# A hand-ordered two-layer attention kernel: a new first image, and small moves in each later turn

## The reference, cut to what matters

```
layer 0, per image x [256, 1024]
  q = Wq x + bq, k = Wk x + bk        (32 rows each)
  v = Wv x + bv                       (256 rows)
  attn = softmax over j of q_i . k_j
  x1 = gamma * (v attn^T) + x
layer 1, per image x1 [256, 1024]
  h = group_norm(x1) (32 groups of 8 channels)
  q, k, v = projections of h (256 rows each)
  attn = softmax(q . k / 16)
  y = x1 + Wproj (v attn^T) + bproj
```

## Time and profile before

| | us |
|---|---|
| median of 3 runs | 840.06 (836.66 to 841.46) |
| the profiled execution, its own time | 842.42 |
| its span in the profile | 840.6 |
| PE busy | 789.0 (94%), 3756 matmuls |
| DVE busy | 556.8 (66%) |
| ACT busy | 471.2 (56%) |
| POOL busy | 166.7 (20%) |

### The profile page before, as it was taken

One profiled execution on the slowest core, in us unless ns is written; L12 is line 12 of the kernel. 1 busy time (PEld: TensorE's weight loads), 2 busy tenths in 40 slices (PEclk: granted clock), 3 DMA queues, 4 the chain that ended last, 5 costly groups with the idle time before them and its releaser, 6 DMA issues.

```text
span 840.6 us, 9682 instructions
## 1 busy us (share of the span) xinstructions
PE 789.0 (94%) x3756; PEld 645.5 (77%) x3756; DVE 556.8 (66%) x787; ACT 471.2 (56%) x609; POOL 166.7 (20%) x141
## 2 busy tenths in 40 slices
PE   5788887999999989999999999999999999999998
PEld 4567666888788777877778877888778788888786
DVE  5554675677758686676956777586865857385665
ACT  4755663557654576445854657545765457444343
POOL 3600233201310041103310034100421024102300
PEclk9879999899999999999999999999999999999999
DMA  7000001001100011000200002000100001000101
GB/s 225 0 1 2 1 0 51 1 1 40 62 1 1 1 51 51 1 1 1 83 19 1 1 0 101 1 1 1 50 1 1 2 1 50 1 1 1 50 1 51
DMA packets 10365, 18.98 MB, mean 23 GB/s; under 512 B 2128, under 2 KB 3920, under 8 KB 10320
## 3 DMA queue, kind: packets, MB, share of 16 engines
q1 hardware_dynamic: 10320, 18.36, 6.3%
HBM read 9.97 MB, written 8.39 MB: 22 GB/s over the span
## 4 chain that ended last, share of the span: by engine, by line
PE 70%; DVE 20%; ACT 7%; issue 2%; DMA 1%; SPq 0%; ACTq 0%; DVEq 0%
PE ring L524 22%; PE ring L526 21%; PE ring L525 21%; PE ring L534 3%; DVE pt_lo L946 3%; PE ring L544 2%; ACT prob L743 2%; DVE neg_raw L931 2%; DVE bn L989 2%; DVE x_lo L861 2%; DVE neg_max L929 2%; DVE pt_lo L949 1%; DVE h_lo L869 1%; ACT ring L764 1%; DVE res L982 1%
## 5 line engine op out<-in xcount | busy, mean ns | idle before, releaser
L524 PE MATMUL ring<-pt_hi,v_hi 128*128 128x512 f32 x512 | 204.1, 399 | 4.2 <-issue 2.0
L525 PE MATMUL ring<-pt_lo,v_hi 128*128 128x512 f32 x512 | 202.6, 396 | 0.0
L526 PE MATMUL ring<-pt_hi,v_lo 128*128 128x512 f32 x512 | 202.5, 395 | 0.0
L743 ACT ACTIVATE prob<-ring,neg_max 128x1024 f32<-128x1024 f32 x64 | 71.6, 1118 | 179.1 <-DVE neg_max L932 179.1
L931 DVE TENSOR_REDUCE neg_raw<-ring 128x1 f32<-128x1024 f32 x64 | 77.9, 1217 | 86.9 <-PE ring L526 86.9
L465 POOL TENSOR_TENSOR v_lo<-v_f,v_hi 128x512 fp32r<-128x512 f32 x32 | 42.9, 1341 | 440.8 <-ACT v_hi L781 440.8
L524 PEld LDWEIGHTS ring<-pt_hi,v_hi 128*128 128x128 f32 x512 | 97.5, 190 | 26.7 <-issue 3.8
L526 PEld LDWEIGHTS ring<-pt_hi,v_lo 128*128 128x128 f32 x512 | 97.6, 191 | 21.8
L525 PEld LDWEIGHTS ring<-pt_lo,v_hi 128*128 128x128 f32 x512 | 97.8, 191 | 19.3
L524 PE MATMUL ring<-h_hi,query_hi 128*128 128x512 f32 x256 | 101.2, 395 | 5.2 <-DVE spread L967 4.9
L929 DVE TENSOR_REDUCE neg_max<-ring 128x1 f32<-128x1024 f32 x64 | 77.7, 1221 | 42.0 <-PE ring L534 42.0
(11 more groups left out here) (118 smaller groups left out, 1234.5 us busy)
## 6 DMA issues: line engine op xcount, KB each, us to landing
out_y<-res SPq DMA_DIRECT2D x32, 256.0 KB, 2.1
x_in<-in_x SPq DMA_DIRECT2D x7, 1024.0 KB, 4.9
x_in<-in_x SPq DMA_DIRECT2D x2, 512.0 KB, 4.7
h_f<-in_wv_t SPq DMA_DIRECT2D x1, 256.0 KB, 5.2
res<-in_wq SPq DMA_DIRECT2D x1, 256.0 KB, 7.3
res<-in_wk SPq DMA_DIRECT2D x1, 256.0 KB, 7.5
res<-in_wv SPq DMA_DIRECT2D x1, 256.0 KB, 7.9
res<-in_wp_t SPq DMA_DIRECT2D x1, 256.0 KB, 7.8
```

The source lines that it names most:

```text
L524: mm(out, w_hi, m_hi, start=first, stop=False)
L525: mm(out, w_hi, m_lo, start=False, stop=False)
L526: return mm(out, w_lo, m_hi, start=False, stop=last)
L743: activation(prob[:, p % PROBS], ring[:, slot], ACT.Exp, bias=neg_max[:, k % 2:k % 2 + 1], accum_out=row_sum[:, k % 2:k % 2 + 1]).then_inc ...
```

## The change

**The first image.** Row tiles of scores are filled without the value quarters 2 and 3 among them; only the four `weights` products stand between them. The value quarters 0 and 1 of image 0 are copied whole by ACT into `v1_f` (a buffer of layer 1 that is free then), and POOL splits them (`first_values0`). POOL writes image 1's split x into `h_hi`, `h_lo`, the place of the normalised input, so it need not wait until image 0's `x_hi` has been read. `split_weights` and `residual0(0)` stand later in POOL's queue. DVE instead of ACT takes the weight products out of PSUM. A step `opening` has an order of its own on ACT and DVE: both halves of `qk` of image 1 share one slot, with shift and keys parts between. In the eight steps of `keys` tiles of image 0 the scores of image 1 stand in `late` instead of `early`, two banks of the value product come before `sides`, and three value quarters (0.3, 1.0, 1.1, written image.quarter) stand in `sides` in the `keys` tile's slot. The `bias` products stand behind the first `keys` tile. The split of image 2's x is put earlier, and its low part on DVE.

**The second image.** The value products of images 0 and 1 are evacuated in the step that finishes them. Statistics and the normalised input of image 0 come one step later; its two group sums share slots with `qk 2.1` and `value0 2.0`.

**In a turn.** `qk(i+1, 0)` goes from `sides` to `late` of step 0; the first bank of the value product of step 3 comes behind `qk(i+1, 1)` instead of ahead of it; `norm` goes from `late` to the end of `sides`.

```diff
-PLACE = {("qk", 1, 0): 0, ("qk", 1, 1): 3}
+PLACE = {("qk", 1, 0): 2, ("value0", 0, 2): 3, ("value0", 0, 3): 0, ("value0", 1, 0): 0, ("value0", 1, 1): 0}
...
-HOST = {("norm", 0, m): ("qk", 2, m) for m in range(2)}
+HOST = {("qk", 1, 1): ("qk", 1, 0), ("bias", 0, 0): ("value0", 0, 2),
+        ("norm", 0, 0): ("qk", 2, 1), ("norm", 0, 1): ("value0", 2, 0)}
...
+    start, scores, opening = Step(slots=(0, 1, 2, 3)), Step(slots=(0, 1, 2)), Step()
+    start.sides = tiles("qk", 0, (0, 1)) + tiles("value0", 0, (0, 1))
+    scores.late = tiles("scores", 0, (0, 1, 2))
+    for m in range(4):
+        scores.late += tiles("weights", 0, (m,)) + tiles("scores", 0, (3 + m,))
+    scores.late += tiles("scores", 0, (7,))
+    scores.take_weights = True
+    opening.opening = True
+    opening.sides = tiles("qk", 1, (0, 1)) + tiles("value0", 0, (2,))
+    opening.late = tiles("shift", 0, (0,))
+    steps = [Step(("keys", 0, k), (0, 0, k - 2) if k >= 2 else None) for k in range(TILES)]
+    steps[0].sides = tiles("bias", 0, (0,))
+    steps[0].rest = True
+    for k in range(7):
+        steps[k + 1].late = tiles("scores", 1, (k,))
+    steps[3].sides = tiles("value0", 0, (3,))
+    steps[4].sides = tiles("value0", 1, (0,))
+    steps[6].sides = tiles("value0", 1, (1,))
+    steps[6].split_x = steps[7].split_x_lo = 2
+    s8, s9, s10 = Step(None, (0, 0, 6)), Step(None, (0, 0, 7)), Step(("keys", 1, 1))
+    s8.early = tiles("scores", 1, (7,))
+    s8.early_log = 1
+    s8.late = tiles("value0", 1, (2,))
+    s9.sides = tiles("shift", 1, (0,))
+    s9.late = tiles("keys", 1, (0,)) + tiles("value0", 1, (3,))
...
-    s3.statistics = 0
+    s4.statistics = 0
     s4.sides = tiles("qk", 2, (0,))
-    s4.late = tiles("norm", 0, (0,))
-    s5.sides = tiles("qk", 2, (1,))
-    s5.late = tiles("norm", 0, (1,))
+    s5.sides = tiles("qk", 2, (1,)) + tiles("norm", 0, (0,))
     s6.early = tiles("scores", 2, (0,))
-    s6.sides = tiles("value0", 2, (0,))
-    s6.hidden = s6.hidden_lo = 0
+    s6.sides = tiles("value0", 2, (0,)) + tiles("norm", 0, (1,))
+    s7.hidden = s7.hidden_lo = 0
...
-        steps[0].sides = tiles("qk", i + 1, (0,))
+        steps[0].late = tiles("qk", i + 1, (0,))
+        steps[3].banks_first = 0
         steps[3].sides = tiles("qk", i + 1, (1,))
...
-            steps[s].late = tiles("norm", i, (m,)) + steps[s].late
+            steps[s].sides += tiles("norm", i, (m,))
...
-            if _layer == 0:
+            if _layer == 0 and _image >= 2:
                 STEPS[_n + 1].evacuate = (_layer, _image)
...
+        def x_split(i):
+
+            return (h_hi, h_lo) if i == 1 else (x_hi, x_lo)
...
+            def first_values0():
+
+                for m in range(2):
+                    two = slice(2 * m, 2 * m + 2)
+                    pool.wait_ge(S["value0_taken"], m + 1)
+                    link(G.tensor_copy(v0_hi[:, two], v1_f[:, m]))
+                    G.tensor_tensor(v0_lo[:, two], v1_f[:, m], v0_hi[:, two].bitcast(F32),
+                                    ALU.subtract).then_inc(S["value0_first"], 1)
...
             small_things()
+            first_values0()
+            first_split_x()
+            bias_rows()
             pool.wait_ge(S["x0_loaded"], 16)
             pool.wait_ge(x_loaded[0], x_loads(0))
             residual0(0)
-            first_split_x()
-            bias_rows()
             split_weights()
-            split_x(2)
...
+            def opening():
+                log_sums(0)
+                for m in range(2):
+                    query_part(("qk", 1, m))
+                shift_rows(("shift", 0, 0))
+                key_part(("qk", 1, 0))
...
+            def opening():
+                key_part(("qk", 1, 0))
+                shifts(0)
+                key_part(("qk", 1, 1))
+                for m in range(2):
+                    query_part(("qk", 1, m))
```

More of the change, by code:

```diff
@@ L111, in second_image @@
+    s9.sides = tiles("shift", 1, (0,))
+    s9.late = tiles("keys", 1, (0,)) + tiles("value0", 1, (3,))
+    return [start, scores, opening] + steps + [s8, s9, s10]
 def second_image():
@@ L137, in second_image @@
     ones[3].late = tiles("scores", 2, (6,))
-    ones[4].sides = tiles("value0", 2, (2,))
-    ones[4].late = tiles("norm", 1, (0,)) + tiles("scores", 2, (7,))
+    ones[4].sides = tiles("value0", 2, (2,)) + tiles("norm", 1, (0,))
+    ones[4].late = tiles("scores", 2, (7,))
     ones[4].log = ones[5].shifts = 2
-    ones[5].sides = tiles("value0", 2, (3,))
-    ones[5].late = tiles("norm", 1, (1,))
+    ones[5].sides = tiles("value0", 2, (3,)) + tiles("norm", 1, (1,))
     ones[6].sides = tiles("shift", 2, (0,))
@@ L521, in wait, with wait_read @@
                 pe.wait_ge(S[name], n)
+            def wait_read(entry):
+                for got in (entry, GUEST[entry]) if entry in GUEST else (entry,):
+                    wait(*reader(got))
+                    if got[0] == "qk":
+                        wait("key_hi", 2 * got[1] + got[2] + 1)
             def three(out, w_hi, w_lo, m_hi, m_lo, first, last):
@@ L658, in fill @@
                 elif kind == "qk":
-                    last = project_qk(i, m, out)
+                    last = project_qk(i, m, half_place(entry))
                 elif kind == "value0":
@@ L687, in values @@
                     elif before and b % 2 == 0:
[L688 to L690 removed]
+                        wait_read(before)
                     w, cols = slice(ct * P, (ct + 1) * P), half_cols[half]
@@ L816, in _ @@
             for now in STEPS:
+                if now.opening:
+                    opening()
+                    continue
                 logits = now.tile and now.tile[0] == "logits"
@@ L1033, in _ @@
                 for entry in now.sides + now.late:
-                    if entry not in first:
+                    if entry not in first and not now.rest:
                         follow(entry)
@@ L1037, in _ @@
                     split_hidden(now.hidden_lo)
+                if now.take_weights:
+                    take_weights()
+                if now.rest:
+                    project_lo(("value0", 0, 2))
+                    project_lo(("bias", 0, 0))
                 if now.shifts is not None:
```

122 lines of the change are left out of this document (67 added, 55 removed).

## The result

The changed kernel takes **847.15 us** (median of 8 runs, 845.10 to 849.36), the kernel before 841.63 us (median of 8 in the same session, 836.66 to 843.48). The ratio is 1.0071 (95%: 1.0047 to 1.0095): slower by 0.7%, or 5.5 us, where 0.2% faster was forecast. The profiled execution took 845.68 us (span 843.9), 3.3 us more than that of before.

A forecast was written before the change was run, and what follows sets the result against it. Bounds: DVE's queue in a turn; in image 0 an ACT-DVE ring around two PSUM slots, and PE's clock. 3.8 + 1.8 - 0.8 - 6.2 - 0.2 = -1.6 us on 842.4 gives 840.8, as median 838.5; range 831 to 846.

The forecast's parts named there:

- The turn: Turns 2 to 6: DVE idles before the first keys tile's low part, 0.76 us a turn, +3.8 us together.
- The second image and the evacuation: Second image -0.8 us, waits going and new ones coming; image 1's evacuation wait gone, -6.2; its first group sum, -0.2.
- the forecast wait of 1.4 us at `scores(2, 0)`: Second image: PE's scores wait for the reader of the first group sum, 1.4 us.
- Opening and keys steps together: Image 0 up to image 1's first value product, 98.05 us in place of 96.24: +1.8 us, bounds -3.1 to +8.5.
- First exponential at 32.65: Opening: eight row maxima in succession end at 26.6, the path behind stays 6.1 us; 32.65 in place of 37.76, -5.1 us.
- The bound of -1 us: Opening's far bound: GpSimd's two subtractions hold DVE up by 2.1 us each, leaving a gain of 1 us.
- GpSimd's chain: Opening: two value quarters, then image 1's x, from 15.4 to 26.2 us, so that `qk(1, 1)` just finds it.
- 4.85 us to the second exponential: Image 0, first to second keys exponential: 4.05 us, 3.57 of them bias products, plus 0.8 for an even chance of half clock.
- Rounds: 43.1 forecast: Image 0's keys steps: three plain 17.1 us, three with a value quarter 20.8, half clock 3.2, image 2's split 2.0.
- Image 0 falls to 1.2 GHz: Slower rival, chance 0.18: PE bounds image 0's plain steps at 7.4 us against 5.7; +6.7 us, 845.2 us.
- The turn is what it looks like: Faster rival, chance 0.12: PE's waits of 1.65 and 0.49 us count fully, five turns win about 8.8 us; 825.9 us.
- The clock holds: Faster rival, chance 0.19: PE stays at 2.4 GHz in image 0 and the second image, 4.9 us off; 833.6 us.

The follow-up runs named there:

- e1: The kernel before with the turn's three moves alone (`qk(i+1, 0)`, the bank, `norm`); 845.95 us, ratio 1.0048.
- e3: The changed kernel with DVE taking a `qk` entry in `late` ahead of the step's tile again, PE's and ACT's orders kept; 844.52 us, ratio 1.0041.
- e12: The kernel before with two moves of the turn alone (`norm`, the bank behind `qk`), the first half of `qk` left in place; 840.19 us, ratio 0.9989.
- e4: The changed kernel with GpSimd's first residual (image 0) waiting until the shift of image 0 is made; 841.66 us, ratio 1.0001.
- e7: The changed kernel with e4's GpSimd wait, scores 1 to 6 of image 1 in `early`, and the turn of before; 825.49 us, ratio 0.9806.
- e9: e7 with the low part of a later image's x on DVE one step earlier in each turn; 818.37 us, ratio 0.9721.
- e10: e9 with the first scores tile of image 1 early too and image 0's statistics back in their old step; 815.15 us, ratio 0.9689.
- e6: The changed kernel with 13 useless matmuls in PE's two opening waits, 8 before the shift, 5 before the first keys tile; 843.92 us, ratio 1.0024.
- e2: The changed kernel with the turn of before, so the new first and second image alone; 844.12 us, ratio 1.0026.
- e11: The changed kernel with the low part of image i+2's x on DVE one step earlier in each turn; 839.31 us, ratio 0.9974.
- e8: The kernel before with the low part of image i+2's x on DVE one step earlier in each turn; 833.05 us, ratio 0.9896.

## Why the prediction was wrong

**The turn: right.** +3.8 forecast, +4.3 in the profiled pair (0.85 for 0.76 us a turn), +4.1 in e1, with DVE's idle 0.76 us just where it was expected. e3 and e12 show the cause: DVE's order for one entry.

**The second image and the evacuation: right in size, and not in every part.** Forecast -0.8, -6.2 and -0.2; measured -1.9 up to 145.97 and -5.95 from there (16.98 us in place of 22.93), in the trace. The wait for the first group sum came as forecast (1.71 us for 1.75), the one at the first query tile was 1.06 for 1.35, one stretch at a lower clock came (0.86 from 118.18 to 130.00), and the forecast wait of 1.4 us at `scores(2, 0)` did not come at all. At the evacuation the two short waits are 0.65 and 0.19 for 0.65 and 0.35.

**Opening and keys steps together: the step that failed.** It was summed at +1.8 and measured at +6.9. By its own terms:

- *First exponential at 32.65: 35.40.* 0.6 of the 2.75 are the maxima's later end (27.24 for 26.6). The path behind them, taken as the old 6.1 us, took 8.2; in e4, e7, e9 and e10 it took 6.05 to 6.06, and 8.05 to 9.35 in every trace where GpSimd did not wait. The difference is the shift's small instructions held by GpSimd. The step compared only the big DVE instructions with GpSimd's queue, and kept the path behind the last maximum "as long as before" without laying the moved `residual0` beside it. The bound of -1 us covered it, but for the wrong instruction. The row maxima were safe, as forecast: eight in 9.63 us, with GpSimd busy beside them. The Trainium skill ("SBUF — State Buffer", Who interferes with whom) says this of `tensor_reduce`, and names casts among the instructions that can take the port which DVE shares with GpSimd. By that rule, the trace agrees on both; I had applied its first half alone. The prediction quoted it for two SBUF inputs too, which the cast's two neighbours have, and did not lay it against them. The same step adds GpSimd's chain wrongly: 15.4 and twice 1.8 and 3.4 make 25.8, not 26.2. It ended at 26.73, and PE had no wait for it.
- *4.85 us to the second exponential: 7.68.* The even chance of half clock, 0.8, was the whole stretch in fact. PE had just waited 1.80 and 1.18 us, and the kernel before worked at 0.50 in the same place, behind its first keys tile; "even" was too kind: all five traces with such waits (1.80 to 2.62 and 1.18 us) and without e6's matmuls show 7.68 us at 0.50. Behind waits of 0.17 to 0.19 and 1.18 us (e4, e7, e9, e10) it was 4.51 to 5.89. e6 shows the price, 3.7 us.
- *Rounds: 43.1 forecast, 42.6 measured.* Plain ones 5.71, 5.62 and 5.68 for 5.7. The three with a quarter took 25.6 together for 26.0, though otherwise shared out: the first two held full clock (7.0 each), the third took 11.56. That the first held it is this execution's luck. e2, e3 and e11 have the same head, and there it took 8.46 to 9.51 us at a clock of 0.80 to 0.65, where half clock had been forecast (6.9 + 1.6). From the last exponential to the first value product of image 1 it was 17.46 for 17.45.

**The rivals.** "Image 0 falls to 1.2 GHz" gave 845.2, near the result, but not by its mechanism. A clock of 0.76 from 33 to 80 us means about 23 us at 0.5, more than the 15 at which it was to decide, so by its own mark it came. But plain rounds still took 5.7 and not 7.4: one of the three was at 0.50, and there ACT and DVE were still just the longer. It charged 5.1 us to the plain rounds, where the half clock cost nothing, and nothing beyond the forecast's 0.8 to the bias products, where PE worked without a gap and it cost 3.7. "The turn is what it looks like" is refuted by e1, and e8 shows what does take PE's 1.65 us wait away. "The clock holds" is refuted by the windows above; e6 bought part of it.

**The size left over.** The profiled pair gives +3.3 and the medians +5.5. The changed kernel's runs lie at 845.1 to 845.7 and at 848.6 to 849.4, and the profiled one is of the first group. What the second does otherwise was not profiled, but e2, e3 and e11 have the same head: their first keys exponential of image 2 comes at 202.95, 203.50 and 202.60, in the changed kernel's profile at 200.52. The head of the kernel before stands in four traces (its own, e1, e8, e12), at 201.53, 200.74, 198.59 and 202.43. The means are 202.4 and 200.8. So the new head costs about 1.6 us and not the -1.0 of the profiled pair, and with 4.3 in the turns that is 5.9 for the measured 5.5.

**The base.** 838.5 was counted from a median of three runs, 840.06. The eight runs beside the changed kernel have 841.63. So of the 8.65 us between 838.5 and 847.15 about 1.6 are the base and 7 the change.

## What to carry to other kernels

Before moving work to another engine's queue, lay the moved instructions beside the small ones on the critical path, not only beside the large ones: here instructions on eight columns were held 1 to 1.5 us each beside GpSimd's work, PE's wait grew by that, and the clock doubled the bill. Where an engine's wait stands in a chain, follow the queue of its releaser back to where that engine last idled, and move work from there: the small waits of 1.65 and 0.49 us could not be won by reordering PE, but went when one low part was taken out of DVE's queue ahead of them. A low clock is free only where other engines' work is the longer, so price it by window and not by image: a plain round took 5.7 us at 0.50 as at 1.00, the bias products 7.68 for 4.01, and the first round with a quarter 8.46 us at 0.80 for 7.01 at 1.00, although PE also waits in it, because there PE's work is a link of the chain. And take a stage's length from more than one execution: this head varied by 3 to 4 us between traces of the same order.

## What the runs showed of the hardware

- Instructions of DVE on 128x8 elements, a cast and two `TENSOR_TENSOR`, took up to 1.72, 1.68 and 1.12 us beside GpSimd's `TENSOR_SCALAR` on 128x1024 and the cast and `TENSOR_TENSOR` behind it, 0.17 each with none beside them. Those held end 0.02 to 0.03 us behind an instruction of GpSimd's (32.00 and 31.98; in e2 31.37 and 31.35, 32.73 and 32.70). The low part of x (two 128x1024 halves) took 3.44 us beside GpSimd's value split, 2.36 alone.
- Behind two waits of 1.80 and 1.18 us PE worked 7.68 us at 0.50. With 13 useless matmuls in those waits the same work took 4.01 us, at 0.98.
- Waits of 2.64 and 1.63 us in the rounds of image 0 left the next stretches at 1.00. The same wait of 3.57 us was followed by 0.70 over the round in the changed kernel and by 0.84 in e3 and e6: the length of a wait alone does not tell.
- One kernel's runs can lie in groups: e4's twelve, at 839.6, 841.7 and 843.9, within 0.3 us each.
